# Two orders in the attention loop of a transformer layer: the transpose, copy and value-matmul groups, and the correction matmul

## The reference

```python
def _L0_attn_ref(x, w_attn, w_proj, embk, embv):      # x: (8, 2048, 1024), 16 heads, d = 64
    q, k, v = jnp.split(x @ w_attn, 3, axis=2)         # then split into heads
    rel = jnp.tril(idx[:, None] - idx[None, :])        # idx = arange(T), distance t - s
    rk = embk[rel]; rv = embv[rel]                     # (T, T, d)
    att = einsum('bhtd,bhsd->bhts', q, k) * scale + einsum('bhtd,tsd->bhts', q, rk)
    att = softmax(where(causal, att, -inf), axis=-1)
    y = einsum('bhts,bhsd->bhtd', att, v) + einsum('bhts,tsd->bhtd', att, rv)
    return y.transpose(0, 2, 1, 3).reshape(B, T, C) @ w_proj

def _L0_ffn_ref(x, Wr, br, W1, b1, W2, b2):            # top 1 of 8 experts, H = 2048
    probs = softmax(tokens @ Wr + br); expert = argmax(probs)
    h = relu(einsum('td,edh->teh', tokens, W1) + b1)
    y = einsum('teh,ehd->ted', h, W2) + b2
    return y[expert] * max_prob

x = x + _L0_attn_ref(_layernorm(x), ...)
x = x + _L0_ffn_ref(_layernorm(x), ...)
```

## Time and profile before

| what | us |
|---|---|
| median of 2 runs | 5021.07 |
| the two runs | 4867.65, 5174.49 |
| profiled execution | 4899.69 |
| its span, first to last instruction, slowest core | 4897.8 |
| spans of the eight cores | 4835.9 to 4897.8 |
| PE busy | 3496.0 (71%) |
| DVE busy | 1329.7 (27%) |
| ACT busy | 1281.3 (26%) |
| POOL busy | 213.5 (4%) |

### The profile page before, as it was taken

One profiled execution on the slowest core, in us unless ns is written; L12 is line 12 of the kernel. 1 busy time (PEld: TensorE's weight loads), 2 busy tenths in 40 slices (PEclk: granted clock), 3 DMA queues, 4 the chain that ended last, 5 costly groups with the idle time before them and its releaser, 6 DMA issues.

```text
span 4897.8 us, 48716 instructions; the slowest of 8 cores (4835.9 to 4897.8 us)
## 1 busy us (share of the span) xinstructions
PE 3496.0 (71%) x16065; PEld 1579.9 (32%) x16065; DVE 1329.7 (27%) x2367; ACT 1281.3 (26%) x2210; POOL 213.5 (4%) x373
## 2 busy tenths in 40 slices
PE   0456667666676566766566119999999999999991
PEld 0222223222233222333232004444444444444440
DVE  0045442444424454344452210001110001110001
ACT  3433333233333333333330422221112221112110
POOL 1100001000010000000000010101010100001003
PEclk9955557555575555755558559999999999999885
DMA  5244443444444444244444131303030303122003
GB/s 131 49 133 128 130 125 90 119 130 133 124 99 125 123 131 129 78 130 124 127 130 149 54 59 25 67 3 69 1 69 1 69 3 67 31 38 52 18 1 133
DMA packets 455409, 415.88 MB, mean 85 GB/s; under 512 B 304464, under 2 KB 353632, under 8 KB 455160
## 3 DMA queue, kind: packets, MB, share of 16 engines
q1 hardware_dynamic: 409856, 336.72, 23.5%
q0 software_dynamic: 45312, 76.06, 9.3%
HBM read 264.16 MB, written 157.29 MB: 86 GB/s over the span
## 4 chain that ended last, share of the span: by engine, by line
PE 58%; DMA 11%; issue 9%; DVE 8%; ACT 6%; SPq 6%; POOL 1%; DVEq 0%; ACTq 0%; POOLq 0%
PE ps_v L61 19%; PE ps_h L61 18%; PE ps_s L61 11%; PE ps_y L61 7%; SPq L61 6%; DMA prevh<-prev_sb 5%; DVE ps_s L61 3%; PE ps_t L61 3%; DVE attT_sb L61 2%; ACT xn_sb L61 1%; DMA xt_sb<-x 1%; ACT prev_sb L61 1%; DMA rel_sb<-prevh 1%; DMA bmath<-att_sb 1%; DMA xt_sb<-x_spill 1%
## 5 line engine op out<-in xcount | busy, mean ns | idle before, releaser
L61 PE MATMUL ps_v<-w_sb,h_sb 128*128 128x512 bf16 x4096 | 907.1, 384 | 34.0 <-ACT h_sb L61 34.0
L61 PE MATMUL ps_h<-xn2T,w_sb 128*128 128x512 bf16 x4096 | 908.0, 385 | 29.1 <-DMA w_sb<-w 29.1
L61 ACT ACTIVATE h_sb<-ps_h,b1c_sb 128x512 bf16<-128x512 f32 x512 | 352.6, 689 | 1486.2 <-PE ps_h L61 1486.2
L61 PE MATMUL ps_y<-attT_sb,vaug_sb 128*66 128x128 bf16 x2176 | 328.6, 304 | 478.3 <-DVE attT_sb L61 471.7
L61 DVE SCALAR_TENSOR_TENSOR acc_sb<-ps_v,g_sb,acc_sb 128x512 bf16<-128x512 f32 x256 | 192.3, 751 | 1682.5 <-PE ps_v L61 1682.5
L61 PEld LDWEIGHTS ps_v<-w_sb,h_sb 128*128 128x128 bf16 x4096 | 402.5, 99 | 538.6 <-issue 107.3
L61 PEld LDWEIGHTS ps_h<-xn2T,w_sb 128*128 128x128 bf16 x4096 | 405.2, 99 | 526.4 <-issue 84.9
L61 ACT ACTIVATE att_sb<-ps_s,cst_sb 128x512 bf16<-128x512 f32 x640 | 397.5, 687 | 677.5 <-DVE ps_s L61 573.3
L61 DVE TENSOR_TENSOR ps_s<-ps_s,rel_sb 128x512 f32<-128x512 f32 (+3 forms) x624 | 387.5, 669 | 238.5 <-PE ps_s L61 161.2
L61 PEld LDWEIGHTS ps_y<-attT_sb,vaug_sb 128*66 128x66 bf16 x2176 | 228.1, 163 | 567.2 <-issue 565.0
L61 DVE COPY attT_sb<-ps_t 128x512 bf16<-128x512 bf16 (+3 forms) x640 | 227.3, 379 | 302.8 <-PE ps_t L61 298.3
(11 more groups left out here) (83 smaller groups left out, 1380.0 us busy)
## 6 DMA issues: line engine op xcount, KB each, us to landing
w_sb<-w POOLq DMA_DIRECT2D x64, 512.0 KB, 13.6
w_sb<-w POOLq DMA_DIRECT2D x128, 256.0 KB, 10.4
prevh<-prev_sb SPq DMA_DIRECT2D x80, 384.0 KB, 2.5
rel_sb<-prevh SPq DMA_DIRECT2D x80, 384.0 KB, 5.4
bmath<-att_sb SPq DMA_DIRECT2D x80, 384.0 KB, 3.2
xt_sb<-x SPq DMA_DIRECT2D x32, 512.0 KB, 4.3
rel_sb<-prevh SPq DMA_DIRECT2D x64, 256.0 KB, 3.8
xt_sb<-x_spill SPq DMA_DIRECT2D x32, 512.0 KB, 3.9
```

What stands on the lines that cost most here:

```text
L61: ins = getattr(h, method)(*args, **kw)
```

## The change

It has two parts. In `trav_closure` the loop over groups is written anew: the transposes of two groups are emitted ahead of the first copy, in the loop the transposes of a group come before the value matmuls of the group two before, and each copy but the first comes after value matmuls and is handed the semaphore value that stands after them (before, that of its own transposes). A strip of one group keeps its order.

In the closures at the end of a block, finb_sb is written by ScalarE from ps_y, right after its copy to fin_sb, and no longer by VectorE from fin_sb; and the correction matmul moves from `fin_closure` to the front of `fin_closure_b`, where it waits for ScalarE's copy.

```diff
--- before.py
+++ after.py
@@ -281,6 +281,7 @@
             fin_pe_guard = [0]
             fin_war_dve = [0]
             fin_rec = [0]
+            fin_fb = [0]
             plast_dve = [0]
             dbg_att_guard = [0]
             prev_free = [0, 0]
@@ -606,12 +607,20 @@
                                                if (i % 4 == 0 and st == 0) else [])),
                                        incs=([(s_pe, 1)] if st == j1 - 1 else []))
 
-                            emit_copy(0, emit_trans(0))
-                            for q4 in range(1, ngr):
-                                pv = emit_trans(q4)
-                                emit_avs(q4 - 1)
-                                emit_copy(q4, pv)
-                            emit_avs(ngr - 1)
+                            pv0 = emit_trans(0)
+                            if ngr == 1:
+                                emit_copy(0, pv0)
+                                emit_avs(0)
+                            else:
+                                emit_trans(1)
+                                emit_copy(0, pv0)
+                                for q4 in range(2, ngr):
+                                    emit_trans(q4)
+                                    emit_avs(q4 - 2)
+                                    emit_copy(q4 - 1, s_pe.n)
+                                emit_avs(ngr - 2)
+                                emit_copy(ngr - 1, s_pe.n)
+                                emit_avs(ngr - 1)
                             att_tr_done[ssl] = s_pe.n
                             vaug_guard[hpar] = s_pe.n
 
@@ -658,22 +667,23 @@
                                           (s_dve, fin_war_dve[0])],
                                    incs=[(s_act, 1)])
                                 fav = s_act.n
-                                EM("vector", "tensor_copy", finb_sb[64:66, 0:512],
-                                   fin_sb[64:66, 0:512], waits=[(s_act, fav)],
+                                EM("scalar", "copy", finb_sb[64:66, 0:512],
+                                   ps_y[ypar][64:66, :], incs=[(s_act, 1)])
+                                finb_av = s_act.n
+                                EM("vector", "reciprocal", fin_sb[64:65, 512:1024],
+                                   fin_sb[64:65, 0:512], waits=[(s_act, fav)],
                                    incs=[(s_dve, 1)])
-                                fdv_cast = s_dve.n
-                                EM("vector", "reciprocal", fin_sb[64:65, 512:1024],
-                                   fin_sb[64:65, 0:512], incs=[(s_dve, 1)])
                                 fin_war_dve[0] = s_dve.n
                                 fin_rec[0] = s_dve.n
+                                fin_fb[0] = finb_av
+
+                            def fin_closure_b(tc=tc, ypar=ypar, h=h,
+                                              fin_rec=fin_rec, fin_fb=fin_fb):
                                 EM("tensor", "matmul", ps_y[ypar][0:64, :],
                                    ev_sb[64:66, :], finb_sb[64:66, 0:512],
                                    start=False, stop=True, skip_group_check=True,
-                                   waits=[(s_dve, fdv_cast), (s_const, CONST_D)],
+                                   waits=[(s_act, fin_fb[0]), (s_const, CONST_D)],
                                    incs=[(s_pe, 1)])
-
-                            def fin_closure_b(tc=tc, ypar=ypar, h=h,
-                                              fin_rec=fin_rec):
                                 rbk = pool_alloc()
                                 rbg = pool_state[rbk]
                                 EM("tensor", "matmul", pool_banks[rbk][0:64, :],
```

## The result

The changed kernel is slower: the ratio of its time to that of the kernel before is 1.0464, 95% interval 1.0399 to 1.0530. The forecast was 1.048 (5133 against 4899.69 us). The profiled execution took 5097.81 us, with a span of 5096.3 us; the lowest times are 5076.06 us after and 4861.44 us before. In some executions, of either kernel, the cores of a die show a lower granted clock and take longer; the comparisons here leave these dies and executions out, so the medians over all (5299.87 us of 11 runs, 4879.56 us of 10) are not set against each other.

What follows compares the result with a forecast made beforehand. Attention was taken as a chain jumping between engines, none of them full, so added waits lengthen the kernel. From 4899.7 us, Part 1 adds 234.9 and Part 2 takes 1.2: 5133 us, 4.8% more, range 5040 to 5255.

Steps and rivals of the forecast that it cites:

- strip 12: First four-group strip of a head's 16: put on the chain in the strip loop, 1.95 us in each of 16 heads.
- Part 2: Finishing blocks: cast off VectorE saves 21.8 us, correction matmul moved to the second block costs 20.6; sum -1.2 us.
- the stall: Old group loop: pause among value matmuls in strips of three and four groups, 0.43 us each, taken off the added cost.
- full wait: Group loop: a four-tile copy now waiting for the previous group's value matmuls, said to add 0.86 us.
- the closed loop: Within an attention strip: scores, adds, copy, value matmuls, next scores; nothing runs ahead, so each added microsecond lengthens the kernel.
- Part 1: Group loop in attention: added copy waits less the old stall, summed over strips and heads, said to cost 234.9 us.
- the drain: Last head's strips 13 to 15, worked off without cover: 6.3 us, plus about 3 us for a possibly lower clock.
- The writing stage: Strips 13 to 15, worked off while the next head writes strips to HBM: 63.5 + 6.1 us, last head apart.
- Hidden in the writing stage: Rival: waits for prevh writes cover the added waits there, taking away 63.5 + 6.1 us: 5064 us; chance 0.12.
- Clock: Rival: new pauses take away TensorE's upper clock level in attention, +175 us, 5308 us; chance 0.04.
- Waits hidden: Rival: DMA or DVE hides the added copy waits, nothing measured, 4900 to 4998 us; chance 0.05.
- PE's 106 us on the chain: Rival: PE's wait for finb_sb before the correction matmul was on the chain, copy waits hidden: 4794 us; chance 0.03.

Runs made afterwards that it cites:

- own_wait: Changed kernel, same new order, but each copy waits only for its own transposes and the value matmuls of the group two before; ratio 0.9943 to the kernel before.
- p1_only: Kernel before with only the new group loop in `trav_closure`, finishing blocks as before; ratio 1.0398 to the kernel before.
- p2_only: Changed kernel with the old group loop, so only the finishing blocks are new; ratio 0.9956 to the kernel before, mean die span 4843.1 us.
- p1_upto12: Changed kernel with the old group loop for strips 13 to 15 of each head; ratio 1.0257 to the kernel before, mean die span 4996.9 us.
- cast_only: Kernel before with finb_sb written by ScalarE from ps_y instead of VectorE's cast, correction matmul left in the first block; ratio 0.9944.
- move_only: Kernel before with the correction matmul moved to the head of the second finishing block, VectorE's cast kept; ratio 1.0020.
- four_slots: own_wait with attT_sb doubled to four group slots, so each copy waits for its own transposes alone; ratio 0.9908 to the kernel before.

## Why the prediction was right

The direction, the place and the price of a wait were right. That the total came within 0.2 points of the measured growth is in part luck: strip 12 was put 23 us too dear and Part 2 10 us, and against them stand the stall, 8 us too cheap, and longer bt stretches, about 10 us, which the sum had at nothing.

- **A wait costs its length.** Forecast 0.86 us for each full wait: drain 0.18, 0.11, copy 0.42, 0.15. The strips of the kernel after give it: from the first value matmul to the next work, strips 4 to 7 grew by 0.66, 0.73, 0.79 and 0.85 us (medians over all cores; forecast 0.66, 0.73, 0.79, 0.86). own_wait shows that it is the wait, and nothing else in the loop.
- **The stall taken off was mis-sized.** I took 0.43 us off each strip of three and four groups, whatever the size of its last group. The stall is the wait of the last copy, so it is shorter when that copy is: from the first work after the copy of group 0 (V0 before, T2 after) to the next work behind the strip, strip 8 took 1.41 us before and takes 2.68 in the kernel after, 1.27 more (medians), where the sum had 1.09. With a stall that shrinks as the copy does, each three-group strip grows by 2 x 0.86 - 0.43 = 1.29 and each four-group one by 2.15. That is 6 us more in the sum for the strips 8 to 11, and 2 for the later ones. The traces have 1.26 to 1.27 us and 2.0 to 2.1.
- **Strip 12 was put on the chain, and is not** in 12 of 16 heads. The step that was wrong is "Strips 0 to 12 are worked off in the strip loop, on the chain". I read the closed loop in the middle of a head and carried it to its last strip, where the chain leaves PE and DVE through the exponentials. It was the same cover that the next sentence found for strip 13. Too much: 16 x 1.95 = 31 us, where four heads give 8.6.
- **Put right**, Part 1 is 16 x (3.04 + 4 x 1.29) = 131.2, strip 12 8.6, strip 13 3 x 2.15 = 6.5, strips 14 and 15 15 x 4.30 = 64.5, the drain 6.5 + 3 = 9.5 (the 3 still the estimate; strips 13 to 15 of the last head grew by 8.5 us in all): 220.3 us. Measured: 218. Summed over the same strips the traces give 215 us (274.3 to 489.5 in p1_only); with the 10 of the bt stretches that is 7 more than was measured, and these 7 are open.
- **The writing stage** was forecast at 79 us with the drain, and 74 to 79 were measured.
- **Part 2**: cast -21.8, measured -23.0; correction matmul +20.6, measured +12.8; sum -1.2, measured -11.3 in p2_only. The sign of the second was right; the term took 0.43 us at 48 places, and only 16 of them show the whole.
- **The rivals.** Hidden in the writing stage: out (p1_upto12). Clock: it was not the cause, since four value matmuls take 0.61 us before and after and own_wait gives the whole loss back, but it was not nothing either (below). Waits hidden: out. PE's 106 us on the chain: out twice, by cast_only, which keeps the wait, and by move_only, which removes it.
- **The clock's share.** The sum had no term for it. A first finishing block, two rows of the kernel before and then two of the kernel after:

```profile
1079.44 3.29 PE L61 MATMUL ps_y<-bt_sb,e_sb 128*66 128x512 bf16 x8
...
1084.38 1.03 PE L61 MATMUL ps_s<-qkv_sb 64*128 64x512 bf16 x4
```

```profile
1015.70 3.62 PE L61 MATMUL ps_y<-bt_sb,e_sb 128*66 128x512 bf16 x8
...
1019.26 1.52 PE L61 MATMUL ps_s<-qkv_sb 64*128 64x512 bf16 x4
```

The mean granted clock over the eight embv matmuls was 0.62 in the first and 0.50, the lower level, in the second: behind group work without the pauses the upper level was granted before they ended, behind group work with them it was not. From first to last start the blocks at strips 11 and 15 took 2.71 and 2.50 us before, 2.95 and 2.95 after (means over all cores), 0.69 us a head or 11 us in all, on the chain that leads through ScalarE's copy to the reciprocal. The kernels with the new waits (after, p1_only) all show it, and own_wait, with the new order and no such pauses, does not (2.61 and 2.47 us). But it is not the pauses alone that move the rise: in four_slots, whose group work is shorter, the block at strip 15 took 2.90 us. The rival's 175 us did not come.
- The sign seen in the profile that I had named wrongly: PE's waits on attT_sb before value matmuls did not grow (468.7 us); the growth is in a row that did not exist before, PE ps_t on attT_sb, 338.7 us. The copy of group 0 is now awaited by T2 and no longer by V0.

## What to carry to other kernels

When a loop is re-ordered and its waits are semaphore counts taken "as of now", look at each count after the move: the copy here needed its own transposes and got the value matmuls emitted in between, and this one number cost 4.5% while the same order, with its own waits and a store of four slots, runs 30 us faster than the old one (four_slots against p2_only). Moving work ahead hides nothing while it waits for the same buffer as the work that it was moved past. And follow the chain at the ends of a loop as well as in its middle: an instruction in the loop's tail can be covered by what the last trip sets off.

## What the hardware showed

- exp(-ln(x)) of 512 values on one partition takes ScalarE 0.58 and 0.72 us, VectorE's reciprocal 3.34 us.
- Two ScalarE copies of 2x512 in a row start 0.49 us apart, though each is shown 0.58 us long.
- 128x128 transposes run at the upper clock level too when it is granted: behind a first block of the kernel after eight took 0.62 us, against 0.76 before and 1.04 at the lower level. It brought nothing, since DVE's reciprocal ends later.
- The same eight 512-column matmuls at strip 15 took 2.50 us from first to last start in the kernel before, where the upper level came in their midst, and 2.95 in the kernel after, where it came behind them.
